# A three-pass attention and feed-forward kernel: the norm and the transposes of each row come in the middle of the row ahead, the weight splits between chunks

## The reference, cut to what matters

```python
xn = layernorm(x)                       # x: 4 rows x 512 tokens x 256; over the last axis
# attention: 16 heads of 128, 4 key/value heads, causal
Q, K, V = xn @ Wq + bq, xn @ Wk + bk, xn @ Wv + bv
attn = softmax(Q @ K.T / sqrt(128) + mask)
y = gelu((attn @ V) @ Wo + bo)          # exact gelu
s = layernorm(xn + y) * gamma + beta
# feed-forward: 256 -> 2 x 1024 -> 256
gate, up = split(xn @ w_gate_up.T)
g = silu((silu(gate) * up) @ w_down.T)
out = x + s * g
```

## Time and profile before

| | |
|---|---|
| median of 3 runs | 715.47 us (715.37 to 715.48) |
| profiled execution | 716.74 us |
| its span, first to last instruction | 714.9 us |
| mean granted TensorE clock | 0.989 |
| TensorE busy | 671.6 us, 94% |
| VectorE busy | 480.0 us, 67% |
| ScalarE busy | 433.2 us, 61% |
| GpSimd busy | 279.7 us, 39% |

### The profile page before, as it was taken

The page is one execution under the profiler, slowest core; times in us unless marked ns, Lnnn a source line. Parts: engine busy times, 40 slices in busy tenths (PEclk is TensorE's granted clock), DMA queues, the critical chain, the costliest instruction groups (busy, mean ns, idle before and its releaser), DMA issues.

```text
span 714.9 us, 11581 instructions
## 1 busy us (share of the span) xinstructions
PE 671.6 (94%) x3968; PEld 585.2 (82%) x3968; DVE 480.0 (67%) x1620; ACT 433.2 (61%) x1011; POOL 279.7 (39%) x328
## 2 busy tenths in 40 slices
PE   1889999999999999999999999999999999999982
PEld 1778888888888888897888888888888897888872
DVE  6764433334776777777868776786768677867777
ACT  3423232326767677668767675867767677767661
POOL 2599100000524324146815242484425146715234
PEclk9799999999999999999999999999999999999998
DMA  8334000002000000000110000002000000200000
GB/s 275 119 129 136 1 29 0 30 0 85 5 1 1 1 0 1 1 1 1 56 34 2 1 1 0 2 1 89 1 1 1 1 1 1 89 1 2 1 1 29
DMA packets 14503, 20.31 MB, mean 28 GB/s; under 512 B 752, under 2 KB 12144, under 8 KB 14192
## 3 DMA queue, kind: packets, MB, share of 16 engines
q1 hardware_dynamic: 13328, 14.37, 6.1%
q0 software_dynamic: 1120, 5.24, 2.2%
HBM read 15.41 MB, written 4.19 MB: 27 GB/s over the span
## 4 chain that ended last, share of the span: by engine, by line
PE 86%; DVE 7%; ACT 4%; issue 1%; DMA 1%; SPq 0%; DVEq 0%; ACTq 0%
PE bank L949 30%; PE down_ps L949 28%; PE down_ps L1048 8%; PE down_ps L987 6%; PE bank L974 6%; PE bank L976 6%; DVE cT_lo L822 2%; PE bank L1035 2%; ACT cT_hi L702 2%; DVE hidT_lo L766 1%; DMA raw<-in_wgu 1%; DVE pT_lo L804 1%; DVE xnT_lo L751 1%; ACT L655 1%; ACT res L655 0%
## 5 line engine op out<-in xcount | busy, mean ns | idle before, releaser
L561 POOL TENSOR_TENSOR probs<-probs,inv 128x512 f32<-128x512 f32 (+3 forms) x256 | 180.7, 720 | 385.0 <-DVE inv L907 384.9
L692 ACT ACTIVATE probs<-probs,least 128x512 f32<-128x512 f32 (+3 forms) x256 | 142.2, 558 | 40.5 <-DVE least L900 36.8
L900 DVE CUSTOM_DVE_ANT_0 probs<-bank,mask 128x512 f32<-128x512 f32 (+3 forms) x256 | 121.2, 486 | 12.1 <-issue 12.0
L804 DVE TENSOR_TENSOR pT_lo<-down_ps,pT_hi 128x512 fp32r<-128x512 f32 x156 | 107.1, 687 | 20.0 <-ACT pT_hi L698 15.4
L698 ACT ACTIVATE pT_hi<-down_ps 128x512 fp32r<-128x512 f32 x156 | 92.5, 593 | 33.1 <-PE down_ps L1048 31.1
L1048 PE MATMUL down_ps<-ident,probs 128*128 128x128 f32 x624 | 93.4, 272 | 0.0
L1048 PEld LDWEIGHTS down_ps<-ident,probs 128*128 128x128 f32 x624 | 75.5, 140 | 12.4
L949 PE MATMUL down_ps<-wo_lo,cT_hi 128*128 128x256 f32 x256 | 73.7, 288 | 6.0 <-DVE cT_lo L822 6.0
L816 DVE SCALAR_TENSOR_TENSOR qT_lo<-bank,bias,qT_hi 128x512 fp32r<-128x512 f32 x64 | 47.5, 750 | 43.5 <-ACT qT_hi L685 43.5
L949 PE MATMUL down_ps<-pT_lo,v_hi 128*128 128x512 f32 x156 | 67.8, 435 | 5.6 <-DVE cT_lo L822 4.2
L949 PE MATMUL down_ps<-wo_hi,cT_lo 128*128 128x256 f32 x256 | 72.0, 281 | 0.0
(11 more groups left out here) (139 smaller groups left out, 1547.6 us busy)
## 6 DMA issues: line engine op xcount, KB each, us to landing
x_row<-in_x SPq DMA_DIRECT2D x4, 512.0 KB, 6.8
raw<-in_wgu SPq DMA_DIRECT2D x4, 512.0 KB, 6.1
raw<-in_wq POOLq DMA_DIRECT2D x2, 1024.0 KB, 5.1
raw<-in_wo POOLq DMA_DIRECT2D x2, 1024.0 KB, 6.2
g_scratch<-g_out SPq DMA_DIRECT2D x4, 512.0 KB, 2.9
x_b<-in_x SPq DMA_DIRECT2D x4, 512.0 KB, 3.7
g_b<-g_scratch SPq DMA_DIRECT2D x4, 512.0 KB, 4.7
out<-res SPq DMA_DIRECT2D x3, 512.0 KB, 2.9
```

The source lines that it names most:

```text
L561: nc.gpsimd.tensor_tensor(p, p, inv[:, u % UNITS, g:g + 1].to_broadcast([P, (tile_of(u) + 1) * P]), ALU.mult).then_inc(probs_made, 1)
L692: nc.scalar.activation(p, p, ACT.Exp, bias=least[:, u % UNITS, g:g + 1], scale=-1.0, accum_out=total[:, u % UNITS, g:g + 1]).then_inc(exp_ ...
L804: nc.vector.tensor_tensor(lo[:], ps, f32(hi[:]), ALU.subtract).then_inc(probsT_split, 1)
L900: nc.vector.tensor_tensor_reduce(out=probs[t][:, g, :], in0=ps[:, 0:(t + 1) * P], in1=mask[:, (T - 1 - t) * P:], scale=-SCALE, scalar=BIG, ...
```

## The change

- Row 0's tokens come in four tiles with a semaphore each, and rows 1, 2 and 3 go into one buffer `x_rows`; row 0 lies in row 3's place, which is loaded again once row 0 is normalised.
- TensorE multiplies a tile of ones 14 times (`clock`) before its first transposes; the products are used by nothing.
- The transposes of a row get banks of their own, `down_ps[:, 2:4]`; the down product uses the first two banks (two token tiles in each).
- Row b+1's statistics come behind chunk 1 of row b on VectorE, its normalisation behind chunk 3, its transposes behind `gate_up(b, 5)`, its high and low parts behind chunk 5.
- The first piece is cut: 128 hidden units of gate and up (4 x 128 columns in two parts of 128 KB) come first, by ScalarE's DMA queue, as the identity does; the rest (two parts of 768 columns) by SyncE's.
- Every high part is made by ScalarE and every low part by VectorE; those of parts 5 to 17 are made behind a given chunk (`parts_at`). GpSimd splits nothing and loads nothing. The wq and wo pieces are cut in two parts of 1,024 columns.
- The loops over rows 1 to 3 on ScalarE and VectorE are written out.

The diff, cut ("..." where lines are left out):

```diff
+CLOCK_RUNS = 14
+TOKENS_AT = 5
+LEAD = 128
...
-    xT_ps = [flat[0:2], flat[2:4],
-             [down_ps[:, 0, :], down_ps[:, 1, :]], [down_ps[:, 2, :], down_ps[:, 3, :]]]
+    down_out = down_ps[:, 0:2, :].rearrange("p a (t d) -> p (a t) d", d=D)
+    xT_ps = [down_ps[:, 2, :], down_ps[:, 3, :]]
...
+    pieces.append([(wgu_v[:, c, :, 0:LEAD], (c * 2 * LEAD, 2 * LEAD, 2),
+                    [gate_up_cols(w, 0, LEAD, c) for w in wgu_s]) for c in range(DC)]
+                  + [(wgu_v[:, c, :, LEAD:half], (DC * 2 * LEAD + c * 2 * rest, 2 * rest, 2),
+                      [gate_up_cols(w, LEAD, rest, c) for w in wgu_s]) for c in range(DC)])
...
-    DVE_PARTS = (0, 4, 5)
-    POOL_PARTS = (1, 2, 3)
+    LEAD_PARTS = DC
+    SPLIT_ORDER = (0, 1, 2, 3, 4, 6, 7, 5)
...
+    def parts_at(b, c):
+
+        order = {(0, 0): 6, (0, 1): 7, (0, 2): 5, (1, 2): 8, (1, 4): 9, (1, 6): 10, (1, 7): 11,
+                 (2, 2): 12, (2, 4): 13, (2, 6): 14, (2, 7): 15, (3, 0): 16, (3, 1): 17}
+        return (order[b, c],) if (b, c) in order else ()
+
+    def split_at(n):
+
+        return SPLIT_ORDER.index(n) + 1 if n < FFN_PARTS else n + 1
...
     @block.sync
...
+        for t in range(T):
+            sp.dma_start(x_rows[:, (B - 2) * T + t, :], x_v[0][:, t, :]).then_inc(x_tile_in[t], 16)
+        load_piece(0, skip=LEAD_PARTS)
+        load_piece(1)
+        sp.sem_inc(g_free, 1)
         load_tokens(1)
...
-        sp.wait_ge(ffn_split_dve, 1)
-        sp.wait_ge(ffn_split_pool, 1)
+        sp.wait_ge(part_split, split_at(3))
         load_piece(2)
+        sp.wait_ge(x_in, 16)
+        load_tokens(2)
+        sp.wait_ge(x_in, 32)
+        sp.wait_ge(xn_made, T)
+        load_tokens(3)
...
+        load_attention(3)
+        load_attention(4)
+        store_g(0)
+        load_attention(5)
+        load_attention(6)
+        store_g(1)
+        load_attention(7)
+        store_g(2)
+        store_g(3)
...
     @block.gpsimd
...
-        root1(0)
-        root1(1)
-        ffn_low(POOL_PARTS[0])
-        root1(2)
-        root1(3)
-        for part in POOL_PARTS[1:]:
-            ffn_low(part)
...
+        for b in range(B):
+            root1(b)
...
     @block.scalar
...
+        act.dma_start(ident[:], ident_in).then_inc(ident_loaded, 16)
+        for src, at, _ in pieces[0][:LEAD_PARTS]:
+            act.dma_start(raw_view(0, at), src).then_inc(lead_in, 16)
         act.wait_ge(table_warm, 1)
         nc.scalar.activation(warm[:], warm[:], ACT.Silu).then_inc(table_warm, 1)
-        ffn_high(0, 1)
+        high(0, 1, 2, 3)
         xT_high(0)
-        xT_high(1)
         gate_part(0, 0)
...
+        high(4)
+        for b in range(B):
             for c in range(FC):
-                if c:
+                if b or c:
                     gate_part(b, c)
+                if b and c == 0:
+                    silu_out(b - 1)
                 hid_high(b, c)
+                high(*parts_at(b, c))
+                if c == TOKENS_AT and b < B - 1:
+                    xT_high(b + 1)
...
     @block.vector
...
+        def low(*which):
             for n, k, at, (hi, lo) in parts():
                 if n in which:
-                    dve.wait_ge(ffn_hi, n + 1)
-                    nc.vector.tensor_tensor(lo, raw_view(k, at), f32(hi), ALU.subtract).then_inc(ffn_split_dve, 1)
+                    dve.wait_ge(part_hi, split_at(n))
+                    nc.vector.tensor_tensor(lo, raw_view(k, at), f32(hi), ALU.subtract).then_inc(part_split, 1)
...
+        def next_tokens(b, c):
+
+            if c == 1:
+                mean_and_variance(b + 1)
+            elif c == 3:
+                normalise(b + 1)
+            elif c == TOKENS_AT:
+                xT_low(b + 1)
+
+        mean_and_variance(0, first=True)
+        normalise(0, first=True)
+        low(0, 1)
         xT_low(0)
...
+        low(2, 3)
         hid_part(0, 0)
...
+        low(4)
+        for b in range(B):
             for c in range(FC):
...
+                if b or c:
+                    hid_part(b, c)
                 hid_low(b, c)
+                low(*parts_at(b, c))
+                if b < B - 1:
+                    next_tokens(b, c)
...
     @block.tensor
...
+            if first and c in (0, 1, FC // 2):
+                pe.wait_ge(part_split, split_at({0: 1, 1: 3, FC // 2: 7}[c]))
...
             for c in range(1, FC):
                 gate_up(b, c, first)
-                if first and c == 1:
-                    transpose_tokens(2)
-                    transpose_tokens(3)
-                    pe.wait_ge(xT_split, B * DC)
+                if c == TOKENS_AT and not last:
+                    transpose_tokens(b + 1)
                 down(b, c - 1, first)
...
+        pe.wait_ge(clock_tile, 1)
+        for _ in range(CLOCK_RUNS):
+            nc.tensor.matmul(gate_ps[1], clock[:, 0:P], clock[:], start=True, stop=True)
         pe.wait_ge(ident_loaded, 16)
-        transpose_tokens(0)
-        transpose_tokens(1)
-        pe.wait_ge(xT_split, 2 * DC)
+        transpose_tokens(0, first=True)
+        pe.wait_ge(xT_split, DC)
         gate_up(0, 0, first=True)
```

More of the change, by code:

```diff
@@ L280, in build @@
     raw = [sb(f"raw{i}", [P, PIECE], F32, early) for i in range(RAW_SLOTS)]
+    x_rows = sb("x_rows", [P, (B - 1) * T, D], F32, early)
+    xn = sb("xn", [P, T, D], F32, early)
+    stats1 = sb("stats1", [P, T, 6], F32, early)
+    ve1 = sb("ve1", [P, T], F32, early)
     first = ExitStack()
[L283 to L286, removed]
+    clock = sb("clock", [P, L], F32R, first)
     first.close()
@@ L333, in transposed @@
         return (ring_ps[slot], qT[slot]) if spare else (probsT_ps[slot], pT[slot])
[L336 removed]
+    x_tile_in = [sem(f"x_tile_in{t}") for t in range(T)]
+    x_in, lead_in, clock_tile = sem("x_in"), sem("lead_in"), sem("clock_tile")
     ident_loaded, const_in = sem("ident_loaded"), sem("const_in")
@@ L414, in parts, with landed @@
                 n += 1
-    def landed(eng, k):
+    def landed(eng, k, lead=False):
+        if lead:
+            eng.wait_ge(lead_in, 16 * LEAD_PARTS)
+            return
         loaded, start = (raw_in, 0) if k < FFN_PIECES else (attn_in, FFN_PIECES)
         eng.wait_ge(loaded[k % RAW_SLOTS], 16 * sum(
-            len(pieces[i]) for i in range(start, k + 1) if i % RAW_SLOTS == k % RAW_SLOTS))
+            len(pieces[i]) - (LEAD_PARTS if i == 0 else 0)
+            for i in range(start, k + 1) if i % RAW_SLOTS == k % RAW_SLOTS))
     banks, banks_last = ring(), ring(last=True)
@@ L445, in _, with load_attention, store_g @@
         sp.dma_start(rowc[:], rows).then_inc(const_in, 16)
-        sp.wait_ge(ffn_split_dve, 1)
-        sp.wait_ge(ffn_split_pool, 1)
+        sp.wait_ge(part_split, split_at(3))
         load_piece(2)
-        sp.sem_inc(g_free, 1)
-        for b in range(B):
+        sp.wait_ge(x_in, 16)
[3 more added lines that the diff above has]
+        load_tokens(3)
+        def load_attention(k):
+            sp.wait_ge(part_split, max(split_at(n) for n, piece, _, _ in parts() if piece == k - RAW_SLOTS))
+            for src, at, _ in pieces[k]:
+                sp.dma_start(raw_view(k, at), src).then_inc(attn_in[k % RAW_SLOTS], 16)
+        def store_g(b):
             sp.wait_ge(g_made, b + 1)
@@ L482, in root1 @@
             pool.wait_ge(var_made, b + 1)
[L483 to L490, removed]
-        root1(0)
-        root1(1)
-        ffn_low(POOL_PARTS[0])
-        root1(2)
-        root1(3)
-        for part in POOL_PARTS[1:]:
-            ffn_low(part)
[L500 to L520, removed]
+            nc.gpsimd.tensor_tensor(norm[:, b * T:(b + 1) * T, 1], ve1[:], neghalf[:], ALU.pow).then_inc(rstd_made, 1)
+        for b in range(B):
+            root1(b)
         def over_tiles(row):
@@ L951, in product, with transpose_tokens @@
             return ins
-        def transpose_tokens(b):
-            pe.wait_ge(xn_made, b + 1)
-            for c in range(DC):
-                for t in range(T):
-                    last = nc.tensor.transpose(xT_ps[b][c][:, t * P:(t + 1) * P],
-                                               xn[:, b % 2, t, c * P:(c + 1) * P], ident[:])
-                last.then_inc(xT_done, 1)
+        def transpose_tokens(b, first=False):
+            if not first:
+                pe.wait_ge(xn_made, b + T)
+                pe.wait_ge(xT_split, b * DC)
+            for t in range(T):
+                if first:
+                    pe.wait_ge(xn_made, t + 1)
+                for c in range(DC):
+                    last = nc.tensor.transpose(xT_ps[c][:, t * P:(t + 1) * P], xn[:, t, c * P:(c + 1) * P], ident[:])
+                    if t == T - 1:
+                        last.then_inc(xT_done, 1)
         def gate_up(b, c, first=False):
```

132 lines of the change are left out of this document (49 added, 83 removed).

## The result

The changed kernel takes 706.71 us (median of 4 runs, 705.39 to 707.49), the kernel before 715.48 in the same set: ratio 0.985, 95% interval 0.9813 to 0.9887. A second set gave 705.78 (6 runs, 705.02 to 707.01). Over all ten runs the median is 706.1. The profiled execution is the fastest of the first set: 705.39, span 703.5; the kernel before had 716.74 and 714.9.

What follows compares the result with a forecast made beforehand. TensorE's order of work was taken to set the end. First key projection: 12.6 + 133.6 + 2.9 + 1.7 + 1.9 = 152.7 us, 12.0 less; 715.47 - 12.0 = 703.5, range 698.5 to 709.0.

Steps and rivals of the forecast that it cites:

- What the work is: Ahead of attention: 17.9 us pass before the feed-forward stage and 13.2 are lost in it; attention's 550.2 stays.
- Start 12.6: Opening: first gate/up matmul at 12.6 us, 5.3 gained, with weights landing at 9.2, after the tokens; bounds 11.3 to 15.
- Clock 1.7: First gate/up group: a pause of 3.0 us probably drops the clock, costing 1.7 us, from 0 to 2.4.
- Transposes 2.9: Feed-forward stage: 24 transposes instead of 16 on TensorE's path, 2.9 us in three lumps of 0.96.
- Splits 0 in rows 1 to 3: Rows 1 to 3: splits on ScalarE and VectorE fit between chunks and cost TensorE nothing.
- Row 0 1.9: Row 0: TensorE waits 0.7 us from chunk 0 and 1.2 from chunk 1, together 1.9, from 0 to 6.
- GpSimd's part goes with its three stalls, 4.2: Feed-forward stage: with GpSimd splitting nothing, three long stalls on hidT_lo, 4.2 us, go.
- Stage: First gate/up group to first key projection: 133.6 us needed, plus transposes 2.9, clock 1.7 and row 0's waits 1.9.
- Sum: First key projection at 152.7 us for 164.7, 12.0 less; profiled execution 704.7, median 1.27 lower, 703.5.
- the first (all well): Opening and row 0: clock held, no row 0 stalls, weights in by 8; 16.5 us less, 699.0; chance 0.16.
- The second (pile-up): Row 0: late pieces cause TensorE pauses; stalls 4 us longer, clock 0.7 more; 708.2; chance 0.19.
- The third, splits on the path: Between chunks: copy and subtraction don't fit, 2.26 us on the path 13 times; 732.9; chance 0.05.

Runs made afterwards that it cites:

- b_fill: Changed kernel with seven more unused matmuls between row 0's transposes and the first gate/up group; 705.37 us.
- f_tokens7: Changed kernel with the next row's transposes and high and low parts at chunk 7 instead of 5; 719.11 us.
- i_third: Changed kernel with the third weight piece loaded into buffers already free, so its load waits for no split; 704.79 us.
- j_fill_third: Changed kernel with the edits of b_fill and i_third together; 702.59 us.
- e_pool_low: Changed kernel with the low parts of attention parts 8 to 17 made by GpSimd, behind the same chunks; 705.18 us.
- l_free1024: Changed kernel with GpSimd copying and subtracting the attention weights as data lands, in parts of 1,024 columns; 713.99 us.
- m_free2048: Changed kernel with GpSimd copying and subtracting the attention weights as data lands, wq and wo in parts of 2,048 columns; 714.12 us.
- k_all: Changed kernel with b_fill, i_third and row 0's token high parts made ahead of those of weight parts 2 and 3; 701.60 us.
- a_no_warm: Changed kernel without the 14 matmuls at the start; 705.94 us beside 705.78 for the changed kernel in the same set.

## Why the prediction was right

The forecast was 703.5 with 698.5 to 709.0; measured 706.7 and 705.8. Step by step:

- *What the work is*: 17.9 + 13.2 us ahead of attention were the whole field. Right: attention 550.20 both times.
- *Start 12.6*: 13.25. The weights end last, as said. They landed 0.6 later. The tokens were late as well: the last tile's statistics began at 6.12, where I had taken 5.2, and the transposes ended at 10.25 and not at 9.6. That is the direction of the 1 us that I named for a second queue beside them; no run here has the tiles without it.
- *Clock 1.7*: 1.7 in the profile, by luck, as said; 1.4 in the second. Nor did the other price that I named, 2.4 for a warm-up without use, come without the warm-up: 3.3 us at half clock, some 1.6 lost. So the warm-up brings nothing, but not for that price. The sentence "it lies wholly on the path" was wrong: b_fill shows that the chain over the third piece stood beside it.
- *Transposes 2.9*: 2.6, 0.88 for a row (39.68 in the chain). Their being hidden at chunk 5 was right, and f_tokens7 shows what it is worth: 13 us.
- *Splits 0 in rows 1 to 3*: right; no TensorE wait behind row 0.
- *Row 0 1.9*: 1.5 (0.55 and 0.92, for 0.7 and 1.2). I put the second to low(7) with the statistics in one place; in i_third and in j_fill_third the pile stayed and only the landing moved, and the wait went, so the landing is needed for it, as much as that pile.
- *GpSimd's part goes with its three stalls, 4.2*: right in sum, no wait is left behind row 0, but the reason was too simple. e_pool_low keeps its subtractions at no cost. And with the norm now in mid-stage, splits on GpSimd as data lands cost 8 (l_free1024, m_free2048) and not 4.
- *Stage*: 140.1 from the first group to the key projection forecast, 140.05 measured. So close only because errors cancel: transposes 0.3 and row 0 0.4 less than forecast, and 0.6 of scattered loss, which I had seen in the kernel before (0.8) and put at nothing.
- *Sum*: key projection 152.7 forecast, 153.3 measured; profiled execution 704.7 forecast, 705.39 measured. The mis-sized term is the last one, from the profiled execution to the median. I took 1.27 off, since before it was that much above its runs; the profiled run of the changed kernel is the fastest of its set. Of the 3.2 us between 703.5 and 706.7, 1.27 is this subtraction, 0.7 the sum itself, and 1.3 the spread of the runs (705.39 to 706.71).
- *Rivals*: the first (all well) asked for the clock held and no waits, 699.0: k_all, which builds nearly that, has 701.6. The second (pile-up) did not come. The third, splits on the path, did not come either: the steps alone in their chunk, of which the statistics with 2.0 us on VectorE are the longest, brought no wait of TensorE. How far over 2.1 a step could go no run shows.

## What to carry over

Ahead of a warm-up, an earlier transfer or a shorter group, see in the chain whether TensorE is in it there: here two paths of nearly equal length ran side by side, and the repairs gave 0.7 and 1.3 us alone, and 3.5 together. Work for a later stage cost nothing here at fixed places between chunks, with the subtractions on VectorE or on GpSimd, and 8 us when GpSimd copied and subtracted as data landed, beside VectorE's reads of SBUF. A wait of some 3 us on TensorE should be counted with the slow clock behind it, here 5.3 us on top of 8.2 for three.

## What was not expected of the hardware

- In these profiles the granted clock reads 1.00 from the start of the span until its first change, whatever it is. The 14 warm-up matmuls stand under 1.00, but take 5.95 us, 0.43 each, the pitch of half clock; in a_no_warm no fall shows at all, while the first group's matmuls take 0.63 and later ones 0.40:

```profile
15.89 0.63 PE L982 MATMUL bank<-xnT_lo,wgu_hi 128*128 128x512 f32 x1
...
16.90 0.40 PE L984 MATMUL bank<-xnT_hi,wgu_lo 128*128 128x512 f32 x1
```

```profile
13.17:16.50 3.33, 3.33 (x8) 2.65 (x9) 1.68 (x2) 0.00 (x0) 0.00 (x0) 1.00 0.29 106
```

  (a matmul at either pitch, and the stretch of the slow ones, whose clock column, third from the end, says 1.00). In the opening go by the matmuls' pitch. It bears on the earlier trace rows too: the 16 transposes that stand under 1.00 there took 3.40 us, and 16 later ones 1.91.
- Short work beside GpSimd is not slowed in proportion, it is held. Of four normalisations of 0.41 us beside a copy of 2.39 and a subtraction of 4.57 one ended with the copy and one with the subtraction; the other two took their 0.41.
- The rest of the first piece landed at 9.81, 9.67, 8.95 and 9.63 in the changed kernel, b_fill, i_third and j_fill_third, which ask for the same transfers ahead of it: 0.9 us of difference that no edit explains.
